# Second layer's value projection in one 512-column unit a tile, and a new layout of the dense work between attention products

## The reference, cut to what matters

```python
x = _layernorm(x + xattn(x, ctx_1024, ctx_1024, Wq, bq, Wk, bk, Wv, bv, We, be))
# x (16, 224, 512), ctx_1024 (16, 750, 512), all weights (512, 512), 16 heads of 32
q = (Q @ Wq + bq); k = (K @ Wk + bk); v = (V @ Wv + bv)
A = softmax(q k^T / sqrt(32)) over the 750 keys
out = (A v) @ We + be
```

## Time and profile before

| | |
|---|---|
| median of 3 runs | 4072.98 us (4071.92 to 4073.93) |
| profiled execution | 4076.45 us, span 4074.7 us |
| mean granted TensorE clock | 0.883 |
| busy share of the span | PE 82%, PEld 62%, DVE 60%, ACT 41%, POOL 25% |

### The profile page before, as it was taken

The page is one execution under the profiler, slowest core; times in us unless marked ns, Lnnn a source line. Parts: engine busy times, 40 slices in busy tenths (PEclk is TensorE's granted clock), DMA queues, the critical chain, the costliest instruction groups (busy, mean ns, idle before and its releaser), DMA issues. The chain is left out here.

```text
span 4074.7 us, 76863 instructions
## 1 busy us (share of the span) xinstructions
PE 3334.7 (82%) x30709; PEld 2518.6 (62%) x30746; DVE 2438.6 (60%) x3679; ACT 1661.5 (41%) x3078; POOL 1008.7 (25%) x866
## 2 busy tenths in 40 slices
PE   0899833298438999999999999959994799999993
PEld 0343411165227888888888888735552699989993
DVE  8669889899744555555555555537766433333333
ACT  2224389787243434443434343322221333333333
POOL 2000022233012343434333434320001122222220
PEclk9999855555768999999999999969996899999997
DMA  4000223332330011111111111031211333333325
GB/s 160 8 1 1 77 85 110 95 100 74 116 121 21 26 35 30 31 30 30 31 38 48 33 31 30 11 76 43 63 42 42 115 87 88 87 88 87 88 46 159
DMA packets 129911, 253.19 MB, mean 62 GB/s; under 512 B 46338, under 2 KB 46338, under 8 KB 125523
## 3 DMA queue, kind: packets, MB, share of 16 engines
q1 hardware_dynamic: 112802, 209.78, 16.6%
q0 software_dynamic: 15744, 37.00, 5.2%
q10 hardware_dynamic: 1072, 2.10, 0.3%
HBM read 158.02 MB, written 76.14 MB: 57 GB/s over the span
## 5 line engine op out<-in xcount | busy, mean ns | idle before, releaser
L1683 DVE TENSOR_REDUCE arena<-psum 112x4 f32<-112x1504 f32 x256 | 441.6, 1725 | 532.3 <-PE psum L1502 532.3
L1406 POOL TENSOR_TENSOR arena<-arena 125x896 f32<-125x896 f32 x128 | 269.8, 2108 | 729.0 <-ACT arena L1646 729.0
L1646 ACT ACTIVATE arena<-psum 125x1792 f32<-125x1792 f32 x192 | 320.2, 1668 | 160.8 <-PE psum L1516 160.8
L1414 POOL TENSOR_TENSOR arena<-arena 125x896 f32<-125x896 f32 x128 | 269.9, 2109 | 225.0 <-ACT arena L1646 219.9
L2649 DVE TENSOR_TENSOR gelu_T_rest<-arena,gelu_T_high 128x384 fp32r<-128x384 f32 (+1 forms) x192 | 104.7, 548 | 269.8 <-ACT gelu_T_high L2595 269.8
L2488 POOL DMA_INDIRECT x_plus_h_rows<-arena x72 | 116.6, 1619 | 600.3 <-DVE arena L2659 590.9
L2510 PE MATMUL psum<-tokens_T_high,w_high 128*128 128x384 f32 (+1 forms) x768 | 255.6, 333 | 1.8 <-DVE tokens_T_rest L2624 1.6
L2512 PE MATMUL psum<-tokens_T_high,w_rest 128*128 128x384 f32 (+1 forms) x768 | 254.9, 332 | 0.0
L2511 PE MATMUL psum<-tokens_T_rest,w_high 128*128 128x384 f32 (+1 forms) x768 | 254.7, 332 | 0.0
L819 ACT ACTIVATE arena<-arena,scales 112x224 bf16<-112x224 uint8 x512 | 238.5, 467 | 2.7
L2590 ACT ACTIVATE arena<-psum 128x384 f32<-128x384 f32 (+1 forms) x192 | 92.6, 482 | 354.6 <-PE psum L2512 353.7
(11 more groups left out here) (383 smaller groups left out, 8771.1 us busy)
## 6 DMA issues: line engine op xcount, KB each, us to landing
arena<-L_ffn_moe_w SPq DMA_DIRECT2D x16, 2048.0 KB, 13.5
arena<-ctx SPq DMA_DIRECT2D x16, 1500.0 KB
arena<-arena SPq DMA_DIRECT2D x16, 896.0 KB, 7.1
arena<-x_after_attn SPq DMA_DIRECT2D x32, 448.0 KB, 16.1
dots_ints<-arena SPq DMA_DIRECT2D x16, 784.0 KB, 4.8
arena_1b<-dots_ints SPq DMA_DIRECT2D x16, 784.0 KB, 5.6
arena<-x SPq DMA_DIRECT2D x7, 1024.0 KB, 14.0
v_ints<-arena SPq DMA_DIRECT2D x32, 224.0 KB, 2.3
```

The source lines that it names most:

```text
L1406: G.tensor_tensor(some_exps[:, r, :, :], prob[:, t, :, 0:NS], prob[:, t, :, NS:2 * NS], ALU.add).then_inc(paired, 1)
L1414: G.tensor_tensor(some_exps[:, 0, :, :], some_exps[:, 0, :, :], prob[:, 1, :, s * NS:(s + 1) * NS], ALU.add).then_inc(paired, 1)
L1646: S.activation(prob[:, t, :, :], score_psum(MC, 2 * NS), ACT.Exp, scale=SCALE2).then_inc(exp_done, 1)
L1683: return V.tensor_reduce(rmx[:, i // 2, i % 2, :], score_psum(HALF, HC), axis=AX.X, op=ALU.max).then_inc(r_free, 1)
```

## The change

A VV unit is now a whole tile: the same 12 weight loads, each with all 512 columns of Wv moving, into a whole PSUM bank; there are 6 units a batch instead of 12, and ACT copies 512 columns at once. In `WINDOWS` all 24 slots are still filled, with the units laid out anew: six VV slots (one with C 7 behind it), two slots of three C units each, and three slots with a single Q unit. The slots with K, O, and with Q 3 and C 0 stay where they were; the C units come earlier in the batch than before.

```diff
-        NV2 = 2 * MT
+        NV2 = MT
         WINDOWS = (
-            (((K, 6),), ((K, 7),), ((Q, 3), (C, 0)), ((O, 0),), ((VV, 0), (C, 1)), ((VV, 1), (C, 2))),
-            (((VV, 2), (C, 3)), ((O, 1),), ((VV, 3), (C, 4)), ((K, 0),), ((VV, 4), (C, 5)), ((VV, 5), (C, 6))),
-            (((VV, 6), (C, 7)), ((K, 1),), ((O, 2),), ((VV, 7), (Q, 0)), ((K, 2),), ((O, 3),)),
-            (((K, 3),), ((VV, 8), (Q, 1)), ((K, 4),), ((VV, 9), (Q, 2)), ((K, 5),), ((VV, 10), (VV, 11))),
+            (((K, 6),), ((K, 7),), ((Q, 3), (C, 0)), ((O, 0),), ((C, 1), (C, 2), (C, 3)), ((VV, 0),)),
+            (((VV, 1),), ((O, 1),), ((C, 4), (C, 5), (C, 6)), ((K, 0),), ((VV, 2), (C, 7)), ((VV, 3),)),
+            (((Q, 0),), ((K, 1),), ((O, 2),), ((VV, 4),), ((K, 2),), ((O, 3),)),
+            (((K, 3),), ((Q, 1),), ((K, 4),), ((VV, 5),), ((K, 5),), ((Q, 2),)),
         )
...
                     elif kind == VV:
                         pe.wait_ge(c_rest, b * NC2 + (i // 2 + 1))
-                        keys, cols = slice(i // 2 * MC, (i // 2 + 1) * MC), slice(i % 2 * DV2, (i % 2 + 1) * DV2)
-                        three(psum[0:MC, at, 0:DV2], lambda k: ctxT_h[:, k, keys], lambda k: ctxT_l[:, k, keys],
+                        keys, cols = slice(i * MC, (i + 1) * MC), slice(0, D)
+                        three(psum[0:MC, at, :], lambda k: ctxT_h[:, k, keys], lambda k: ctxT_l[:, k, keys],
                               lambda k: Wh["v"][:, k, cols], lambda k: Wl["v"][:, k, cols]).then_inc(v_mm, 1)
...
                         act.wait_ge(v_mm, b * NV2 + (i + 1))
-                        S.copy(vR[:, u, i // 2, i % 2 * DV2:(i % 2 + 1) * DV2], psum[0:MC, at, 0:DV2]).then_inc(v_moved, 1)
+                        S.copy(vR[:, u, i, :], psum[0:MC, at, :]).then_inc(v_moved, 1)
```

## The result

The changed kernel takes 4092.96 us (median of 5 runs, 4091.05 to 4098.3) against 4073.93 us before (median of 5 runs, 4071.92 to 4078.94): ratio 1.0046, 95% interval 1.0034 to 1.0058, slower by 19 us. Forecast were 4090 us, 17 us more, with a range of 4079 to 4099.

A forecast was written before the change was run, and what follows sets the result against it. TensorE's issued work was taken to bound layer 2, with five changed slots now waiting for the maximum or exponential. 15 batches at 1.14 us, 17.1, less 0.45 before the loop, gave about +17 us: 4090 us, range 4079 to 4099.

The forecast's parts named there:

- The bound: Layer 2 batch: TensorE's issued work sets the time, but slots under a maximum or exponential last at least 1.81 to 1.90 us.
- The wide unit: 512-column value products in layer 2: 0.227 us apart, 2.92 us a lone unit, the form alone saving 0.65 us a batch.
- 215.7 ns at 512 columns: Trainium skill's measured distance between back-to-back matmul starts; by it the kernel would be only about 5 us slower.
- The sum: Whole kernel: 15 batches at 1.14 us more, 17.1 us, less 0.45 before the loop, about +17 us.
- the preparation of batch 0: Before the loop: 144 products become 72, 0.65 us less, a longer last copy takes about 0.2: -0.45 us.
- What I cost at nothing: Layer 2's ACT copies, DVE's subtractions behind three C units, and SP's loads: no added time.
- The copy of 512 columns: ACT's copy at a value slot's end: taken as 0.6 us, delaying the next exponential only beyond 1.0.
- The bank cover: After three C units, the first bank is free at 2.56 us, TensorE asks at 2.94: 0.38 us to spare.
- SP's loads: Next context's loads wait for the store behind O 3, so C 7 coming earlier issues no transfer earlier; no cost.
- Wider products did save: Rival: wider products pay and nothing waits in layer 2's slots; -9 us, 4064 us; chance 0.04.
- run at their floor: Rival: wide value products take 0.213 us each; +2 us, 4075 us, no change; chance 0.08.
- The clock did not fall: Rival: TensorE's clock falls after three-C slots with a wait; 45 us more, 4135 us; chance 0.06.

## Why the prediction was right

**The bound.** That a slot lasts at least as long as the maximum or exponential over it held to a hundredth: 1.90, 1.81 and 1.85 us were read from bare slots of the first and last batch, and these are the lengths of the five short slots. Half the maximum shortens exactly the three that lie under a maximum; more products fit free of charge into the three Q slots, and not into a full one. That is shown, not argued. For the two slots under an exponential it is the added products and the view of waits that show it; no run made the exponential shorter.

**The wide unit.** The direction of the term was right, the size was not. I took 0.227 us from layer 3's rows; it is 0.232. Six units of twelve products make 72 x 0.005 = 0.36 us a batch, and this is the whole of the miss, 1.47 us a batch measured (91.89 - 90.42) against 1.14 forecast. The gain of the form alone is then 144 x 0.118 - 72 x 0.232 = 0.29 us, half of the 0.65 I had; the order before with wide products measured 0.32. About half of the 5 ns I could have read before. Rows 5 begin at the ninth product of a run of 24; the second to the seventh of that run lie farther apart:

```profile
3315.60 0.39 PE L2511 MATMUL psum<-w_rest,gelu_T_high 128*128 128x512 f32 x1
...
3316.76 0.39 PE L2510 MATMUL psum<-w_high,gelu_T_high 128*128 128x512 f32 x1
```

That is 1.16 / 5 = 0.232 us. Over the 46 such runs of layer 3 in the trace before, the distances from the second to the twelfth product are 0.2295 us on average and the later ones 0.227, and a value unit has only twelve products. What makes the rest is open: not the weights' 125 columns (tried), and hardly traffic of the attention products, as the 72 products before the loop, with none around them, lie on average 0.233 apart as well. The prediction says that the trace does not agree with 215.7 ns at 512 columns. That holds for these fp32r products; layer 1's bf16 products of 512 columns lie 0.216 us apart in the same trace.

**The sum.** Fourteen batches in step give 14 x 1.47 = 20.6 us in the profiled executions. Batch 0, which I counted like the others, went the other way: 110.73 to 107.17 us. Its five short slots wait as in the other batches, which adds 1.5 us; fewer stretches at the lower clock gave back about 5.0 (the last section). The three parts outside the loop's step add up to -1.6: the preparation of batch 0 gave -0.4 (forecast -0.45), layer 1, with code that is unchanged, -2.7, and all from batch 15 on +1.4. The span grew by 20.6 - 3.6 - 1.6 = 15.4 us, the medians by 19: the profiled execution of the kernel before lay 2.5 us above its median, that of the changed one 1.1 below. So the hit at 17 is partly luck: a value unit 0.06 us longer than taken, and a first batch that ran at a higher clock, cancelled.

**What I cost at nothing.** The copy of 512 columns took 587 ns (0.6 taken), and no exponential waited for it. The bank cover held: no wait at VV 0 or K 0; in batch 1 the bank was free 0.51 us before VV 0 started, where I had 0.38. SP's loads caused none either.

**The rivals.** Wider products did save, but the waits decided. They did not run at their floor. The clock did not fall in batches 1 to 14: the 28 three-C slots with their waits left it at 1.00, which goes with what the transposes before the loop had shown. The rule of the Trainium skill ("TensorE: Matmul & The Clock Gate", "Part 4: PE-mode transpose"), that transposes do not count as busy in the same way and full clock does not engage, I had weighed as a rival; these fp32 transposes, at 1.00, do not agree with it.

## What to carry to other kernels

Where two engines take turns over one buffer, the work put between the turns has a least length, and it is the other engine's time plus two signals (here 0.12 + 1.73 + 0.05 us). Read that length where the slot happens to be empty, at the first or last turn of a loop, and add up the slots as the larger of work and least length: a larger unit that saves time by itself loses it again when it can no longer be split to fill all slots. If the larger form is wanted, split it in the other direction (here by the contraction, two slots into one bank), so that every slot keeps its work.

## What the runs showed that was not expected

A pause of 1.8 us is not always followed by the lower clock. Batch 0 has, in every kernel here, a stretch of 10 to 14 us at a granted clock of 0.50 (1.2 of 2.4 GHz) near its start, and four pauses of TensorE later, in the slots without O (each 1.8 us; one of them is 1.05 us with half the maximum). In the kernel before, a stretch at 0.50 followed each of the four: the first in rows 10, the other three here.

```profile
1280.40:1283.70 3.30, 3.30 (x21) 2.85 (x18) 1.73 (x1) 0.00 (x0) 1.78 (x1) 0.50 0.00 0
1307.70:1311.00 3.30, 3.30 (x17) 3.30 (x17) 0.00 (x0) 1.41 (x2) 2.10 (x1) 0.50 0.53 161
1317.90:1321.20 3.30, 3.30 (x44) 1.68 (x40) 2.27 (x4) 0.00 (x0) 1.63 (x1) 0.50 0.02 5
```

In the changed kernel, the windows around and behind its first two pauses, which end at 1259.74 and 1276.87 us, show full clock. After the third the clock fell, and after the fourth, which ends at 1314.62, it stayed at 1.00:

```profile
1259.00:1262.30 3.30, 2.21 (x24) 1.72 (x24) 1.73 (x2) 1.86 (x4) 2.37 (x2) 1.00 0.00 0
1262.40:1266.00 3.60, 3.60 (x43) 2.99 (x44) 1.65 (x3) 1.94 (x2) 2.40 (x2) 1.00 0.00 0
1273.70:1277.00 3.30, 1.53 (x38) 1.03 (x40) 0.94 (x2) 2.25 (x2) 0.02 (x1) 1.00 0.00 0
1277.10:1280.40 3.30, 2.86 (x56) 2.37 (x52) 2.70 (x3) 1.56 (x4) 1.99 (x1) 1.00 0.02 5
1304.00:1307.30 3.30, 3.30 (x23) 2.42 (x12) 0.00 (x0) 1.66 (x1) 0.92 (x1) 0.50 0.00 0
1317.40:1321.00 3.60, 3.60 (x52) 2.78 (x41) 2.06 (x4) 0.34 (x1) 0.00 (x0) 1.00 0.00 0
```

One such fall costs a value unit 1.1 us, and what else runs in the stretch some more. Batch 0 had one fall in place of four and is 3.6 us shorter although its short slots add 1.5 us, so three falls less gave back about 5.0 us, 1.7 us each (an estimate from these differences). The number of falls is not fixed by the order of the slots or the width of the units: with the new order and wide units it was one in the changed kernel, with 128 columns of weights and with six products more in the full slot, but two with six more in the short slots; with narrow units in the new order it was two, and with wide halves in the order before two. Each is one profiled execution, and what decides is open.
